# Causal attention with a linear side branch: score matmuls as four strips of 32 stationary columns, another order of the shifts' work, and programs without loops

## The reference

```
Q, K, V = heads(xn @ wq.T), heads(xn @ wk.T), heads(xn @ wv.T)   # 16 heads of 8 channels
Q, K    = rope(Q), rope(K)
attn    = softmax(causal(Q @ K.T / sqrt(8)))
y       = x + (attn @ V) @ wo.T + xn @ CB.T * (SCB / 127) + bias
```

## Time and profile before

| | |
|---|---|
| median of 3 runs | 287.1 us (285.83 to 287.21) |
| profiled execution | 285.84 us |
| its span, first to last instruction | 284.1 us |
| mean granted TensorE clock | 0.985 |
| TensorE matmul busy | 254.6 us, 90% |
| VectorE busy | 217.6 us, 77% |
| ScalarE busy | 186.5 us, 66% |
| GpSimd busy | 108.0 us, 38% |

### The profile page before, as it was taken

One profiled execution on the slowest core, in us unless ns is written; L12 is line 12 of the kernel. 1 busy time (PEld: TensorE's weight loads), 2 busy tenths in 40 slices (PEclk: granted clock), 3 DMA queues, 4 the chain that ended last, 5 costly groups with the idle time before them and its releaser, 6 DMA issues.

```text
span 284.1 us, 6851 instructions
## 1 busy us (share of the span) xinstructions
PE 254.6 (90%) x1734; PEld 111.1 (39%) x1760; DVE 217.6 (77%) x618; ACT 186.5 (66%) x350; POOL 108.0 (38%) x179
## 2 busy tenths in 40 slices
PE   0695849679999999999999999999999999998984
PEld 0342815333334334432433343334334432464553
DVE  5898368999898888979897898889888979732123
ACT  0326343566778868787777777687868786677851
POOL 6616999838625104500430043025104500640020
PEclk9999799999999999999999999999999999999996
DMA  7514767400660500150033004200500000001011
GB/s 200 179 35 132 212 132 151 119 2 4 141 155 25 155 16 1 45 125 1 0 85 85 0 1 119 51 0 10 157 4 0 1 1 0 3 20 39 18 39 37
DMA packets 22614, 17.76 MB, mean 63 GB/s; under 512 B 4148, under 2 KB 21940, under 8 KB 22600
## 3 DMA queue, kind: packets, MB, share of 16 engines
q1 hardware_dynamic: 22024, 17.00, 23.6%
q10 hardware_dynamic: 576, 0.59, 0.9%
HBM read 12.12 MB, written 5.24 MB: 61 GB/s over the span
## 4 chain that ended last, share of the span: by engine, by line
PE 77%; DVE 8%; DMA 4%; SPq 3%; issue 2%; POOL 2%; ACT 1%
PE psV L841 25%; PE psB L817 24%; PE psA L796 21%; DVE prod L665 4%; PE psA L891 3%; DMA k_scratch<-ot 2%; SPq L273 2%; DMA x_sb<-x 1%; DVE xn L623 1%; SPq L287 1%; DMA ks<-k_scratch 1%; PE psA L910 1%; PE psB L778 1%; DVE prod L650 1%; DVE stats L613 1%
## 5 line engine op out<-in xcount | busy, mean ns | idle before, releaser
L665 DVE CUSTOM_DVE_ANT_0 prod<-psA,cmask 128x128 f32<-128x128 f32 (+7 forms) x256 | 180.5, 754 | 34.4 <-PE psA L796 32.9
L564 ACT ACTIVATE ring<-psB 128x512 f32<-128x512 f32 x288 | 156.6, 602 | 53.7 <-PE psB L817 52.5
L796 PE MATMUL psA<-ks,qs 128*128 (+4 forms) x375 | 88.3, 327 | 9.3 <-DVE mx L665 5.9
L433 POOL TENSOR_SCALAR_AFFINE_SELECT ring<-ring 128x512 f32<-128x512 f32 x64 | 42.1, 670 | 138.5 <-ACT ring L564 138.3
L817 PE MATMUL psB<-qs,ks 128*128 (+4 forms) x367 | 92.6, 326 | 1.6 <-issue 1.1
L841 PE MATMUL psV<-ring,va 128*32 128x512 f32 (+3 forms) x768 | 78.5, 496 | 0.6 <-ACT ot L571 0.6
L817 PEld LDWEIGHTS psB<-qs,ks 128*128 (+1 forms) x384 | 33.2, 97 | 69.9 <-issue 28.7
L796 PEld LDWEIGHTS psA<-ks,qs 128*128 (+1 forms) x384 | 33.1, 98 | 40.2 <-DVE mx L665 11.1
L841 PEld LDWEIGHTS psV<-ring,va 128*32 128x32 f32 x768 | 16.8, 108 | 29.7 <-issue 19.2
L665 DVE DVE_READ_ACCUMULATOR2_ANT mx<- 128x1 f32 x256 | 21.3, 83 | 0.0
L713 DVE TENSOR_TENSOR xn<-psA,x_sb 128x256 f32<-128x256 f32 x6 | 2.5, 425 | 16.1 <-PE psA L910 16.1
(11 more groups left out here) (80 smaller groups left out, 153.4 us busy)
## 6 DMA issues: line engine op xcount, KB each, us to landing
qs<-q_scratch SPq DMA_DIRECT2D x48, 96.0 KB
ks<-k_scratch SPq DMA_DIRECT2D x48, 96.0 KB
q_scratch<-ot SPq DMA_DIRECT2D x20, 128.0 KB, 2.4
k_scratch<-ot SPq DMA_DIRECT2D x12, 128.0 KB, 2.4
x_sb<-x SPq DMA_DIRECT2D x4, 256.0 KB, 4.8
rope_sb<-rope SPq DMA_DIRECT2D x2, 512.0 KB, 6.2
qs<-shiftsT SPq DMA_DIRECT2D x64, 2.0 KB
y<-xn SPq DMA_DIRECT2D x8, 128.0 KB, 1.8
```

The costliest lines, as they stand in the source:

```text
L433: pool.affine_select(out=view, in_=view, compare_op=ALU.is_ge, fill=0.0, base=0, pattern=[[0, QUAD], [1, P]], channel_multiplier=-1).then_ ...
L564: act.activation(ring[:, s % P_RING, k * HALF:(k + 1) * HALF], bank_b(n % B_RING), ACT.Exp)\
L665: last = dve.tensor_tensor_reduce(masked_scores[:, u % 2, at:at + w], psA[:, (u % 2) * SEQ + at:(u % 2) * SEQ + at + w], cmask[:, SEQ - w: ...
L796: mm = pe.matmul(psA[:, (u % 2) * SEQ + at + k:(u % 2) * SEQ + at + min(k + HALF, w)], stack(qs, i, j, t * P, P), stack(ks, i, j, k, min(H ...
```

## The change

- Each score matmul of both passes becomes four, each with 32 of the 128 stationary columns, into 32 PSUM partitions (score_tile). The columns that stream are the same.
- All loops are unrolled; slots, addresses and awaited values are constants, and the semaphore increments that went with register waits are gone. The stacks' loads have semaphores of their own for each slot.
- The order: the units of the next quad and the values steps get other banks; eight units of quad 0 move into the first body, and there units of quad 1 wait for bank 9; POOL's split_maxima(i, 1) moves from between mask(i-1, 8) and mask(i-1, 9) to behind mask(i, 0); turn_shifts(i, 1) moves from unit 1 to unit 2 of the next quad; the tasks change places; the rotation and splitting of the second sequence move from before the first body into bodies 0 to 2; the early output pieces begin at bank 10 instead of bank 1; add_ffn is done in four pieces in body 1; the pads of slot 2 are written before the first body.

```diff
-UNIT_BANK = [1, 2, 4, 6, 7, 9, 10, 12, 14, 15, 15, 19, 20, 21, 23, 24, 25, 26, 27, 30, 32, 34]
-VALUE_BANK = [9, 14, 17, 20, 23, 25, 31, 35, 39, 42]
-LAST_VALUE_BANK = [9, 12, 14, 17, 20, 24, 28, 33, 37, 39]
+UNIT_BANK = [0, 1, 2, 5, 6, 9, 9, 10, 12, 14, 15, 17, 18, 20, 21, 23, 24, 25, 27, 28, 31, 31]
+FIRST_UNIT_BANK = [-1] * 14 + [2, 3, 5, 7, 7, 9, 9, 9]
+VALUE_BANK = [10, 13, 16, 20, 23, 26, 30, 33, 38, 42]
+LAST_VALUE_BANK = [10, 12, 15, 20, 22, 25, 28, 33, 37, 39]
...
-EARLY = {1: 0, 6: 1, 12: 2, 18: 3, 24: 4, 29: 5}
+EARLY = {10: 0, 14: 1, 18: 2, 22: 3, 26: 4, 29: 5}
...
-TASK_AFTER = {1: (3, 0), 2: (3, 1), 5: (4, 0), 6: (4, 1), 7: (5, 0), 8: (5, 1), 11: (6, 0), 12: (6, 1), 13: (7, 0), 14: (7, 1)}
+TASK_AFTER = {0: (3, 0), 1: (3, 1), 3: (4, 0), 4: (4, 1), 5: (5, 0), 6: (5, 1), 8: (6, 0), 9: (6, 1), 11: (7, 0), 12: (7, 1)}
```

SyncE's order from the first body on:

```diff
+            store_shifts(0, 0)
+            load_stack(2, 0)
+            load_stack(2, 1)
+            store_shifts(0, 1)
+            for i in range(1, QUADS):
+                store_shifts(i, 0)
+                store_shifts(i, 1)
+                if i in (1, 2):
+                    store_parts(i + 1)
+                if i + 2 < QUADS and i + 2 >= SLOTS:
...
+                    sp.wait_ge(b_filled, i * NBANKS)
+                    load_stack(i + 2, 0)
+                    load_stack(i + 2, 1)
```

POOL's body, before (first lines) and after:

```diff
-                copy_v(i, 0)
-                mask(i, 0)
-                mask(i, 1)
-                wait(pool, pv_done, i * NSTEPS)
-                copy_v(i, 1)
-                mask(i, 2)
-                if more:
-                    split_maxima(i + 1, 0)
...
-                mask(i, 7)
-                mask(i, 8)
-                if more:
-                    split_maxima(i + 1, 1)
-                mask(i, 9)
+            for i in range(QUADS):
+                wait(pool, pv_done, i * NSTEPS - 3)
...
+                copy_v(i, 0)
+                mask(i, 0)
+                if i > 0:
+                    split_maxima(i, 1)
...
+                mask(i, 1)
...
+                wait(pool, pv_done, i * NSTEPS)
+                copy_v(i, 1)
+                mask(i, 2)
+                if i == 0:
+                    split_maxima(0, 1)
...
+                if i + 1 < QUADS:
+                    split_maxima(i + 1, 0)
...
+                mask(i, 7)
...
+                mask(i, 8)
...
+                mask(i, 9)
```

VectorE and TensorE:

```diff
+            for i in range(QUADS):
                 for u in range(NUNITS):
-                    if u == 1:
-                        turn_shifts(i, 1)
-                    if u == HALF_UNITS + 2:
-                        turn_shifts(i + 1, 0)
-                    maximum(i + 1, u)
+                    if u == 2 and i > 0:
+                        turn_shifts(i - 1, 1)
+                    if u == HALF_UNITS + 3:
+                        turn_shifts(i, 0)
+                    maximum(i, u)
+            turn_shifts(QUADS - 1, 1)
...
+            def score_tile(psum, at, size, keys, queries):
+
+                for strip in range(0, P, STRIP):
+                    mm = pe.matmul(psum[strip:strip + STRIP, at:at + size], keys[:, strip:strip + STRIP], queries,
+                                   start=True, stop=True)
+                return mm
...
-                        mm = pe.matmul(psA[:, (u % 2) * SEQ + at + k:(u % 2) * SEQ + at + min(k + HALF, w)],
-                                       stack(qs, i, j, t * P, P), stack(ks, i, j, k, min(HALF, w - k)),
-                                       start=True, stop=True)
+                        size = min(HALF, w - k)
+                        mm = score_tile(psA, (u % 2) * SEQ + at + k, size, stack(qs, i, j, t * P, P), stack(ks, i, j, k, size))
...
-                    mm = pe.matmul(out_bank[:, col:col + size], stack(ks, i, j, b * P, P),
-                                   stack(qs, i, j, hf * HALF + q0, size), start=True, stop=True)
+                    mm = score_tile(bank_b(n % B_RING), col, size, stack(ks, i, j, b * P, P), stack(qs, i, j, hf * HALF + q0, size))
...
-                        if more:
-                            for u in range(NUNITS):
-                                if UNIT_BANK[u] == n:
-                                    scores(i + 1, u)
+                        for u in range(NUNITS):
+                            if i == 0 and FIRST_UNIT_BANK[u] == n:
+                                scores(0, u)
...
+                        for u in range(NUNITS):
+                            if not last and max(UNIT_BANK[u], 0 if i else FIRST_UNIT_BANK[-1]) == n:
+                                scores(i + 1, u)
```

More of the change, by code:

```diff
@@ L238, in attention_ffn_kernel, with wait, stack_loaded @@
         y_out = sem("y_out")
[L239 to L251, removed]
+        def wait(eng, semaphore, value):
+            if value > 0:
+                eng.wait_ge(semaphore, value)
+        def stack_loaded(i):
+            return 16 * (2 * PARTS * (i // SLOTS + 1) + i // SLOTS)
         SHIFT_DMAS = 4
@@ L389, in leave @@
                 pool.tensor_tensor(raw(c, 1), raw(c, 0), part(c, 0), ALU.subtract).then_inc(late_rest, 1)
[L391 to L398, removed]
+            third_part(0)
+            third_part(1)
+            third_part(2)
+            third_part(3)
+            pads(qs, 2, 0.0, pads_ready)
+            pads(ks, 2, TWO_ONES, pads_ready)
             for half in range(2):
@@ L404, in split_maxima @@
                 n = 2 * i + hf
[L405 to L409, removed]
+                pool.wait_ge(a_drained, i * NUNITS + (NUNITS if hf else HALF_UNITS))
+                wait(pool, shift_turned[hf], i)
                 pool.tensor_scalar(shifts[:, hf, 0:16], mx[:, hf, :], -1.0, None, ALU.mult).then_inc(split_step, 1)
@@ L586, in copy_turned @@
                 act.activation(onT[:, g % 2, :], result_bank(g, 2)[:, 0:2 * P], ACT.Copy).then_inc(onT_ready, 1)
-            body(0, True)
-            with act.Fori(1, QUADS - 1) as i:
-                body(i, False)
             last = QUADS - 1
+            for i in range(last):
+                body(i)
             def beside(n):
@@ L660, in maximum @@
                 t, heads = UNITS[u]
[L661 removed]
+                dve.wait_ge(a_filled, i * NUNITS + u + 1)
                 for j in heads:
@@ L843, in values, with body @@
                 mm.then_inc(pv_done, 1)
-            def body(i, first, more, then=None):
+            def body(i, then=None):
+                last = i == QUADS - 1
                 for s in range(NSTEPS):
@@ L849, in body @@
                         shifted(i, s, k)
[L850 to L853 removed]
+                        for u in range(NUNITS):
+                            if i == 0 and FIRST_UNIT_BANK[u] == n:
+                                scores(0, u)
+                            if i > 0 and UNIT_BANK[u] == NBANKS + n:
+                                scores(i, u)
+                        for u in range(NUNITS):
+                            if not last and max(UNIT_BANK[u], 0 if i else FIRST_UNIT_BANK[-1]) == n:
+                                scores(i + 1, u)
                         for v in range(NSTEPS):
[L855 removed]
+                            if (LAST_VALUE_BANK if last else VALUE_BANK)[v] == n:
                                 values(i, v)
[L857 removed]
+                            elif VALUE_BANK[v] == NBANKS + n and i > 0:
                                 values(i - 1, v)
@@ L865, in _ @@
             pe.wait_ge(products, 8)
-            for u in range(NUNITS):
+            for u in range(FIRST_UNIT_BANK.count(-1)):
                 scores(0, u)
@@ L870, in _ @@
             pe.wait_ge(task_saved, len(TASKS))
-            body(0, True, True)
-            with pe.Fori(1, QUADS - 1) as i:
-                body(i, False, True)
+            for i in range(QUADS - 1):
+                body(i)
             def turn(g, m, quads=range(4)):
@@ L925, in _ @@
             pe.wait_ge(cb_scaled, 4)
-            body(QUADS - 1, False, False, then=early)
+            body(QUADS - 1, then=early)
             values(QUADS - 1, NSTEPS - 2)
```

238 lines of the change are left out of this document (108 added, 130 removed).

## The result

The changed kernel takes 311.99 us (median of 4 runs, 308.23 to 314.0), the kernel before beside it 286.91 us (285.83 to 287.21): a ratio of 1.084, 95% interval 1.073 to 1.094. It is 25 us slower. Ratios here rest on fast runs alone: the run of 314.0 us, and two of the four of the experiment e5, were slow ones. The prediction said slower, 299 us, with a range of 274 to 307: the sign and the mechanism held, the size didn't, and the time lies 5 us outside the range. The span of the profiled execution is 310.8 us against the 297.5 of my sum.

A forecast was written before the change was run, and what follows sets the result against it. TensorE bounds the kernel, 26.58 us a body. Second body at 85, six bodies of 27.5, last body 34.8 plus 1.2 for the clock, tail 11.5: span 297.5; with 1.7 around it 299 us, range 274 to 307.

The forecast's parts named there:

- The chain of the shifts: Steady body: bank 3, mask, split, transpose, landing; bank 10 starts 9.8 us in instead of 5.85, 4.0 us late.
- One sign that I had named: Each body: bank 10's matmul some 9.5 to 10 us after bank 0's, released by the landing of the shifts.
- Rival 2: Shifts of half 1 are there in time: bodies of 24 us, about 273 us; 0.19 with cases between.
- I add nothing and keep up to 1.7 us a body for the range.: Clock after the 2.8 us pause ahead of unit 4 in each other body: no charge, up to 1.7 us in the range.
- that case: Lower clock in most bodies: five bodies at 1.7 us more, near 307 us; chance 0.08.
- The last body: From its start to bank 35: shifts land at 8.4 us, 34.8 us in all, plus 1.2 for the lower clock.
- The second body's start: Prologue and first body: first body starts near 51, shifts land at 67.7, second body starts at 85 us.
- the tail: Time after the last body's bank 35: unchanged at 11.5 us.
- Parts 1 and 2: Four 32-column strips per score tile gain up to 2.3 us a quad; unrolled programs gain up to 1.1 us.
- The change of form: TensorE switching between scores and values: 0.23 us for each of ten values blocks, 2.3 us a body.
- rival 3: Strip loads are bare: 0.1 us more per tile, 77 us, about 375 us in all; chance 0.02.
- the registers: Loop register instructions on TensorE's sequencer: 1.1 us a body, removable by unrolling.

The follow-up runs named there:

- e5: Changed kernel with VectorE's turn_shifts(i - 1, 1) at unit 4 instead of unit 2, split still late: 314.39 us, 1.092 of the kernel before.
- e1: Changed kernel with only split_maxima(i, 1) moved back ahead of copy_v and mask(i, 0): 293.46 us, 1.023 of the kernel before.
- e9: Changed kernel with split_maxima(i, 1) early and the old places for next-quad units, values steps and turn_shifts: 285.96 us, 1.000 of the kernel before.
- e4: Kernel before with its five loops unrolled and each score tile as four strips, order kept: 276.12 us, 0.963 of the kernel before.
- e6: Changed kernel with the early split and the last body's output pieces begun at bank 1 again: 289.99 us, 1.016 of the kernel before.
- e3: Kernel before with its five loops unrolled and nothing else: 282.74 us, 0.988 of the kernel before.
- e7: Kernel before, unrolled and with strips, but full 128-column score matmuls in the last body: 273.84 us, 0.959 of the kernel before.

## Why the prediction was right in kind and wrong in size

**The chain of the shifts held, link by link, but for the last wait.** Bank 3 at 2.85 us (I had 2.9), mask at 3.96 (4.07), split at 4.56 (4.7), transpose at 5.49 (5.7), bank 10 released by the landing at 9.54 in e5 (9.8). One sign that I had named was not there: in the changed kernel's bodies 1 to 6 bank 10 shows no wait for the landing. I had split the 4.0 us into 2.8 ahead of unit 4 and the rest at bank 10. The stop of 2.34 us ahead of unit 4 was the whole of it; behind it TensorE had work until the landing or later, and bank 10 started at 9.53 us in body 2, at the full clock, and at 10.04 to 10.41 in bodies 3 to 6, at the lower. Moving the split alone gave 18.5 us back. Rival 2 is refuted by the same rows: no link was shortened. Its time, about 273 us, is near what the gains gave without the late chain in the old order, 276.12 us.

**The step that failed: "I add nothing and keep up to 1.7 us a body for the range."** The pause was 2.34 us, shorter than my 2.8 and than both pauses that I had compared it with, and still the lower clock followed it in bodies 3 to 6. By the two bodies of e5 it costs 1.70 us. Bodies 3 to 6 took 29.31, 28.72, 29.31 and 28.73 us, 6.1 us above four times 27.5, the largest single part of the 13.3. Not all of it need be the clock: body 2, at the full clock and less its other stop of 1.81 us, took 28.2, by which 3.3 of the 6.1 are the clock's, while by e5's 1.70 all of them are. The share between these stays open. I had written down a price near the measured one and given that case a chance of 0.08. Even that case ends near 307, so the terms below were needed too. From two pauses of the prologue, one of 2.92 us with and one of 2.77 us without the lower clock, I had made a line between them, where the rows allow none.

**A step that had no price.** Bodies 1 and 2, which had no lower clock, were charged like the others, though the diff moves the second sequence's rotation and splitting into them. In body 2 TensorE stops for another 1.81 us, at 132.27, behind that work. Bodies 1 and 2 came out 3.6 us above the sum. With the shifts in time they stand 5.5 us above the steady ones in e1, and 10 in e9, part of that by the lower clock. I had asked where the first body starts (51.69, predicted 51), and not what the moved operations do in GpSimd's order, which was the question I had put to the split itself.

**The last body** was 2.6 us longer. Bank 10 came at 8.96 us (8.4). After it stood two stops of 0.76 and 0.91 us behind VectorE's normalised output, where I had 0.5 for small waits, and the lower clock cost 1.5 instead of 1.2: from bank 10 to bank 35 took 29.6 us here and 28.1 in e1, where its pause was shorter.

**The second body's start** (85, measured 86.6) and the tail were near. The shifts of the first body were to land at 67.7, and its bank 10 started at 67.8. Of the 1.6 us, 0.7 stood ahead of the body (51.69, predicted 51). The lower clock from 66.5 to 69.5 us, which the sum leaves out, can be the rest; no run shows this body without it.

**Parts 1 and 2.** The change of form was right (2.3, measured 2.16), strips of the same length as full tiles were right, rival 3 is refuted, and the registers were worth 0.5 and not 1.1 us a body. The terms cancel within the forecast since the body was built from bank 10 on, not from 26.58 down. That the new places of units, values steps and transposes cost 1.3 us a body, once the shifts are in time, I hadn't seen: it was hidden behind the late landing.

**The sum of causes.** Four kernels in a row lead from before to the changed one, by their ratios to before. Unrolled programs and strips alone give 0.963 (e4). With the rest of the change, but the early split and the old places, it is 1.000 (e9). The new places make it 1.023 (e1), the late split 1.084. In us these steps are -10.6, +10.7, +6.5 and +17.4, which is 24; the medians say 25. The second step isn't parted in full: the later output pieces are 3.7 us of it (by e6). The rest lies in bodies 0 to 2. By the profiles e9 starts its first body 10 us earlier than e4, but takes 9 us more for it and 6 us more for body 2.

## What to carry to other kernels

When an operation moves in an in-order program, follow every chain that stands behind it until it reaches the bounding engine: here three GpSimd operations of 0.25 us each, put behind one mask, cost 18.5 us with the clock that fell behind the pauses, because the mask waits for four exponentials and a transpose, four DMA issues and their landing follow. A pause of the bounding engine is to be priced with the lower clock behind it as a case of real weight, in every body that has the pause. Take a change with many parts apart before it is judged: its two best parts alone were 3.7% faster, within the whole they were lost.

## What the runs showed of the hardware

- The same pause can be followed by either clock. Pauses of 2.34 us (changed kernel, bodies 3 to 6) and 2.05 us (e5) were followed by a stretch at the lower level, while pauses of 2.34 and 2.35 us in bodies 1 and 2, and one of 2.04 us in e5's next body, were not. In bodies 3 and 5 the granted level was already down before the pause ended (in body 3: 1.00 from 151.2 to 151.5 us, 0.50 from 151.6 to 151.9, the pause until 151.92). In bodies 4 and 6 it fell 1.1 us after the end. A price from one pause doesn't carry over to the next.
- Four strips of 32 columns stream as fast as one tile of 128: a body of 480 loads and 480 matmuls took 23.91 us (e4), 25 ns for each instruction, with TensorE busy for 20.00 of 20 us.
- Going over to a values block's form and back cost 0.22 us for each block (2.16 us for ten, e3 to e4).
- The landing of one and the same store can differ between executions: the last store of the second sequence's parts took 3.50 us in e4's profile and 2.47 us in e7's, and TensorE waited 3.36 and 0.67 us behind it.
